# Attention block in fp32: Q and K as two fp32r parts on four 32-row tiles instead of three bf16 parts on two 64-row tiles, with the order of the scores and of the start changed

## The reference, cut to what matters

```python
def tc_rmsnorm(x, t, gw, gb, bw, bb):
    return (t @ gw.T + gb)[:, None] * x * rsqrt(mean(x * x, -1) + 1e-6) + (t @ bw.T + bb)[:, None]

h = tc_rmsnorm(x, cond, g1w, g1b, b1w, b1b)
q, k, v = h @ Wq.T, h @ Wk.T, h @ Wv.T          # 16 heads of 8
p = softmax(q @ k.T / sqrt(8))
x1 = x + (p @ v) @ Wo.T
h2 = tc_rmsnorm(x1, cond, g2w, g2b, b2w, b2b)
out = x + x1 + (silu(h2 @ gate.T) * (h2 @ hid.T)) @ out_w.T
```

## Time and profile before

| | us |
|---|---|
| median of 3 runs | 257.58 (257.5 to 257.66) |
| the profiled execution, its own time | 257.42 |
| its span in the trace | 255.6 |
| PE busy | 221.2 (87%) |
| DVE busy | 202.9 (79%) |
| ACT busy | 163.3 (64%) |
| POOL busy | 111.9 (44%) |

### The profile page before, as it was taken

One profiled execution on the slowest core, in us unless ns is written; L12 is line 12 of the kernel. 1 busy time (PEld: TensorE's weight loads), 2 busy tenths in 40 slices (PEclk: granted clock), 3 DMA queues, 4 the chain that ended last, 5 costly groups with the idle time before them and its releaser, 6 DMA issues.

```text
span 255.6 us, 8235 instructions
## 1 busy us (share of the span) xinstructions
PE 221.2 (87%) x3048; PEld 177.9 (70%) x3048; DVE 202.9 (79%) x490; ACT 163.3 (64%) x352; POOL 111.9 (44%) x183
## 2 busy tenths in 40 slices
PE   2436777879989999899989999999999999899894
PEld 2314545547667868786878877887888778687894
DVE  4646966897899889889988998899888997565673
ACT  5354658676876686669766777567757655666430
POOL 8323852597265254625381516252623232323320
PEclk9995579999999999999999999999999999999998
DMA  5866601530261026100540045004500000000001
GB/s 162 345 169 147 185 4 28 152 85 3 64 166 27 26 64 164 47 23 19 140 124 0 27 112 152 10 27 114 156 6 26 4 26 3 23 3 24 22 21 44
DMA packets 18819, 18.79 MB, mean 74 GB/s; under 512 B 3644, under 2 KB 17980, under 8 KB 18652
## 3 DMA queue, kind: packets, MB, share of 16 engines
q1 hardware_dynamic: 18252, 17.80, 24.7%
q10 hardware_dynamic: 528, 0.46, 0.8%
HBM read 3.22 MB, written 2.10 MB: 21 GB/s over the span
## 4 chain that ended last, share of the span: by engine, by line
PE 45%; issue 24%; POOL 16%; DVE 9%; ACT 4%; ACTq 1%; POOLq 0%; DVEq 0%
PE proj L489 7%; PE pv L427 6%; PE ffn L320 5%; PE ffn L322 3%; PE ffn L321 3%; PE score L410 3%; DVE nmax L756 3%; POOL inv L923 3%; PE raw L383 3%; POOL qp L915 2%; PE tok L442 2%; POOL xn_lo L936 2%; POOL kp L915 2%; POOL xs L929 2%; PE proj L349 2%
## 5 line engine op out<-in xcount | busy, mean ns | idle before, releaser
L756 DVE TENSOR_REDUCE nmax<-raw 128x8 f32<-128x1024 f32 x61 | 74.2, 1216 | 3.0 <-PE raw L383 2.9
L597 ACT ACTIVATE p_s<-score 128x1024 f32<-128x1024 f32 x64 | 65.5, 1023 | 16.1 <-PE score L410 14.9
L427 PE MATMUL pv<-p_s,va 128*32 128x128 f32 x1024 | 41.7, 280 | 1.8 <-ACT xn L615 1.1
L320 PE MATMUL ffn<-xn_hi,ffn_hi 128*128 128x256 f32 x106 | 34.8, 328 | 1.2 <-POOL xn_lo L936 1.2
L626 ACT ACTIVATE th<-ffn 128x256 f32<-128x256 f32 x53 | 20.3, 384 | 19.6 <-PE ffn L322 19.6
L489 PE MATMUL proj<-ffn_out_s,hT 128*128 128x128 f32 x240 | 31.6, 275 | 0.0
L813 DVE SCALAR_TENSOR_TENSOR gated<-th,ffn 128x256 f32<-128x256 f32 x53 | 22.0, 415 | 12.1 <-ACT th L626 11.7
L427 PEld LDWEIGHTS pv<-p_s,va 128*32 128x32 f32 x1024 | 24.7, 109 | 9.2 <-issue 4.0
L936 POOL TENSOR_TENSOR xn_lo<-xn,xn_hi 128x128 fp32r<-128x128 f32 x32 | 14.7, 460 | 34.6 <-DVE xn_hi L804 34.6
L322 PE MATMUL ffn<-xn_hi,ffn_lo 128*128 128x256 f32 x106 | 29.7, 280 | 0.0
L321 PE MATMUL ffn<-xn_lo,ffn_hi 128*128 128x256 f32 x106 | 29.6, 279 | 0.0
(11 more groups left out here) (130 smaller groups left out, 456.0 us busy)
## 6 DMA issues: line engine op xcount, KB each, us to landing
...
qs<-shift SPq DMA_DIRECT2D x64, 4.0 KB
...
```

What stands on the lines that cost most here:

```text
L320: pe.matmul(dst, w_hi, v_hi, start=True, stop=False)
L427: mm = pe.matmul(pv[VW * j:VW * j + VW, (t % 2) * L:(t % 2 + 1) * L], va[vbuf(g)][:, t // 2, at:at + VW], p_s[:, (BEATS * g + t) % PBUF, p ...
L597: act.activation(p_s[:, n % PBUF, :], score[:], ACT.Exp, scale=SCALE).then_inc(s_exp, 1)
L756: dve.tensor_reduce(heads[:, :, t % 2, :], raw_dst(g, t)[:].rearrange("l (e j m) -> l e j m", e=HALVES, j=HQ), AX.X, ALU.max, negate=True) ...
```

## The change

Q and K are split in two fp32r parts, and three products are stacked: 24 of 32 rows, partition stride 4, in tiles of 32 rows. Even steps use tiles 0 and 1, odd steps tiles 2 and 3. The constant `RAW` goes from -7 to -5, so that a raw step has the parity opposite to the score step of its beat, and from beat 3 on their matmuls are issued in turn, one score, one raw, after the waits of both. `a_middle`, `a_lowest` and two buffers go. A group has 6 transfers of 256 KB. The shift is one fp32r row: one copy in `b_shift`, two DMAs for half a group. The transposed maxima go to the `raw` bank, `MAXT` from -3 to -2, and every fourth raw step waits for the shift copy. The first two batches have a maximum transpose, copy and DMA each (`b_first_maxT`, `b_first_shift`, `first_shift_rows`). `tok` and `ffn` become halves of one tensor `aux`, so that raw steps of the first group can use it. The order ahead of the loop changes on all engines; the clearing of `va[0]` moves from DVE to POOL, and the split of the feed-forward weights from beats 4 and 5 to ahead of the loop. The host orders the heads of Wq and Wk to fit. The core of the diff:

```diff
...
-    PARTS = 3
-    Q_PART = [0, 0, 0, 1, 1, 2]
-    K_PART = [0, 1, 2, 0, 1, 0]
+    PARTS = 2
+    TILES = 4
+    TROWS = 32
+    STRIDE = 4
+    Q_PART = [0, 0, 1]
+    K_PART = [0, 1, 0]
...
-    HALF_ROWS = 64
-    RAW_ROWS = 62
+    RAW_ROWS = TROWS - 1
     SHIFT = RAW_ROWS
...
-    RAW, MAXT = -7, -3
+    RAW, MAXT = -5, -2
+    APART = 3
...
-    SPREAD = BEATS * G + RAW + 1 - FFN
+    SPREAD = BEATS * G + MAXT + 1 - FFN
...
-        qp = sb("qp", [D, 2, PARTS, W], BF16)
-        kp = sb("kp", [D, 2, PARTS, W], BF16)
-        q_rest = sb("q_rest", [D, W])
-        k_rest = sb("k_rest", [D, W])
-        qs = [sb(f"qs{u}", [128, HH, W], BF16) for u in range(NBUF)]
-        ks = [sb(f"ks{u}", [128, HH, W], BF16) for u in range(NBUF)]
+        qp = sb("qp", [D, 2, PARTS, W], F32R)
+        kp = sb("kp", [D, 2, PARTS, W], F32R)
+        qs = [sb(f"qs{u}", [128, HQ, W], F32R) for u in range(NBUF)]
+        ks = [sb(f"ks{u}", [128, HQ, W], F32R) for u in range(NBUF)]
         va = [sb(f"va{u}", [L, NB, HALVES * VROW]) for u in range(VBUF)]
...
-        tok = bank("tok")
-        ffn = bank("ffn")
+        aux = bank("aux", 1024)
+        ffn, tok = aux[:, 0:512], aux[:, 512:1024]
...
         def raw_dst(g, t):
-            return score if g == 0 and t % 2 and t < BEATS - 1 else raw
+            return (raw, score, aux, raw, aux, raw, aux, raw)[t] if g == 0 else raw
+        def raw_free(g, t):
+            return BEATS * g + t if g > 0 else (0, 0, 0, 1, 3, 4, 5, 6)[t]
+        def first_maxT(b):
+            return proj[0:H, 0:L] if b == 0 else pv[0:H, 3 * L:4 * L]
...
-                        sp.dma_start(dst[buf(g)][r::DH, :, :].rearrange("p h w -> p (h w)"),
-                                     parts[:, g % 2, part, :]).then_inc(s_stack[buf(g)], 16)
+                        sp.dma_start(dst[buf(g)][r::STRIDE, :, :].rearrange("p j w -> p (j w)").bitcast(F32),
+                                     parts[:, g % 2, part, :].bitcast(F32)).then_inc(s_stack[buf(g)], 16)
             def shift_rows(g, half):
+                sp.wait_ge(s_shift, 2 * g + half if g > 0 else half)
                 for b in range(MB):
-                    for i, ready in enumerate((s_shi, s_slo)):
-                        sp.wait_ge(ready, 2 * g + half + 1)
-                        sp.dma_start(qs[buf(g)][SHIFT + i::HALF_ROWS, :, (MB * half + b) * L:(MB * half + b + 1) * L],
-                                     shift[H * b:H * (b + 1), half, i, :]).then_inc(
-                                         s_shiftrow[buf(g)][MB * half + b], 16)
+                    sp.dma_start(qs[buf(g)][SHIFT::TROWS, :, (MB * half + b) * L:(MB * half + b + 1) * L].bitcast(F32),
+                                 shift[H * b:H * (b + 1), half, :].bitcast(F32)).then_inc(
+                                     s_shiftrow[buf(g)][MB * half + b], 16)
+            def first_shift_rows(b):
+                sp.wait_ge(s_shift0, b + 1)
+                sp.dma_start(qs[0][SHIFT::TROWS, :, b * L:(b + 1) * L].bitcast(F32),
+                             shift_first[:, b, :].bitcast(F32)).then_inc(s_shiftrow[0][b], 16)
...
                 stack_rows(g, ks, kp, K_PART, 0, s_khi)
-                if g == 0:
-                    stack_rows(g, ks, kp, K_PART, 1, s_kmid)
-                    stack_rows(g, ks, kp, K_PART, 2, s_klo)
-                    stack_rows(g, qs, qp, Q_PART, 1, s_qmid)
-                else:
-                    stack_rows(g, qs, qp, Q_PART, 0, s_qhi)
-                    stack_rows(g, ks, kp, K_PART, 1, s_kmid)
-                    stack_rows(g, ks, kp, K_PART, 2, s_klo)
-                    stack_rows(g, qs, qp, Q_PART, 1, s_qmid)
-                stack_rows(g, qs, qp, Q_PART, 2, s_qlo)
+                stack_rows(g, ks, kp, K_PART, 1, s_klo)
+                stack_rows(g, qs, qp, Q_PART, 0, s_qhi)
+                stack_rows(g, qs, qp, Q_PART, 1, s_qlo)
...
-            stack(1)
-            shift_rows(0, 0)
+            one_rows(0)
+            one_rows(1)
+            stack_rows(0, ks, kp, K_PART, 0, s_khi)
+            stack_rows(0, ks, kp, K_PART, 1, s_klo)
+            stack_rows(0, qs, qp, Q_PART, 1, s_qlo)
+            stack_rows(1, ks, kp, K_PART, 0, s_khi)
+            first_shift_rows(0)
+            stack_rows(1, ks, kp, K_PART, 1, s_klo)
+            stack_rows(1, qs, qp, Q_PART, 0, s_qhi)
+            stack_rows(1, qs, qp, Q_PART, 1, s_qlo)
+            first_shift_rows(1)
...
+            def first_key():
+                pe.wait_ge(s_wlo, 1)
+                for n in range(2):
+                    half = slice(2 * n * L, 2 * (n + 1) * L)
+                    pe.wait_ge(s_lo1, n + 1)
+                    mm = split_product(key_dst(0)[:, half], qk_hi[:, 1, :], qk_lo[:, 1, :], xn1_hi[:, half],
+                                       xn1_lo[:, half])
+                mm.then_inc(s_k, 1)
...
+                if raw_free(g, t) > 0:
+                    pe.wait_ge(s_max, raw_free(g, t))
+                if g > 0 and t % HQ == 0:
+                    pe.wait_ge(s_shift, 2 * g - 1 + t // HQ)
...
+            def b_raw_two(g, t):
+                raw_ready(g, t)
+                raw_ready(g, t + 1)
+                for j in range(HQ):
+                    for e in range(HALVES):
+                        first = raw_pair(g, t, e, j)
+                        if j == HQ - 1 and e == HALVES - 1:
+                            first.then_inc(s_raw, 1)
+                        second = raw_pair(g, t + 1, e, j)
+                second.then_inc(s_raw, 1)
...
+            def c_score_and_raw(g, t, f, r):
+                score_ready(g, t)
+                raw_ready(f, r)
+                for j in range(HQ):
+                    for e in range(HALVES):
+                        mm = score_pair(g, t, e, j)
+                        if j == HQ - 1 and e == HALVES - 1:
+                            mm.then_inc(s_score, 1)
+                        nn = raw_pair(f, r, e, j)
+                nn.then_inc(s_raw, 1)
+            def b_maxT(g, half):
+                pe.wait_ge(s_max, BEATS * g + HQ * (half + 1))
+                pe.transpose(raw[:, 0:L], nmax[g % 2][:, half * 128:half * 128 + 128],
+                             ident[:]).then_inc(s_maxT, 1)
+            def b_first_maxT(b):
+                pe.wait_ge(s_max, 2 * (b + 1))
+                if b == 0:
+                    pe.wait_ge(s_va, 1)
+                else:
+                    pe.wait_ge(s_klo, 2)
+                pe.transpose(first_maxT(b), nmax[0][:, H * b:H * (b + 1)], ident[:]).then_inc(s_maxT0, 1)
             def c_pv(g, t, T):
...
-            a_key(0)
+            first_key()
             a_query(0)
             for b in range(NB):
                 a_transpose(1, b)
+            a_values(0)
+            b_raw_two(0, 0)
             a_key(1)
+            b_raw_two(0, 2)
+            b_first_maxT(0)
+            for b in range(NB):
+                a_transpose(2, b)
             a_query(1)
-            b_raw(0, 0)
-            b_raw(0, 1)
-            b_raw(0, 2)
-            b_raw(0, 3)
-            b_raw(0, 4)
-            b_maxT(0, 0)
-            b_raw(0, 5)
-            a_transpose(2, 0)
-            a_transpose(2, 1)
-            a_values(0)
-            a_transpose(2, 2)
-            b_raw(0, 6)
-            a_transpose(2, 3)
             for T in range(LAST + 1):
                 for g, t in due(T, 0, BEATS):
-                    c_score(g, t)
-                for g, t in due(T, RAW, BEATS):
-                    b_raw(g, t)
+                    if T >= APART and due(T, RAW, BEATS):
+                        c_score_and_raw(g, t, *due(T, RAW, BEATS)[0])
+                    else:
+                        c_score(g, t)
+                if T == 0:
+                    b_first_maxT(1)
+                    b_raw_two(0, HQ)
                 for g, t in due(T, PV, BEATS):
                     c_pv(g, t, T)
+                if 0 < T < APART:
+                    for g, t in due(T, RAW, BEATS):
+                        b_raw(g, t)
...
-            a_middle(0, s_krest, k_rest, kp, s_kmid)
             a_high(0, s_q, query_dst(0), qp, s_qhi)
-            a_norm(1, 0)
-            a_norm(1, 1)
-            a_middle(0, s_qrest, q_rest, qp, s_qmid)
             stack_high_queries()
-            a_norm(1, 2)
-            a_norm(1, 3)
+            for b in range(NB):
+                a_norm(1, b)
+            a_values(0)
+            a_mean(2)
+            zero_fill(va[1][:].rearrange("l b v -> l (b v)"), s_va0[1])
             a_high(1, s_k, key_dst(1), kp, s_khi)
+            a_mean(3)
+            for b in range(NB):
+                a_norm(2, b)
             a_high(1, s_q, query_dst(1), qp, s_qhi)
-            a_middle(1, s_krest, k_rest, kp, s_kmid)
-            a_middle(1, s_qrest, q_rest, qp, s_qmid)
-            a_mean(2)
-            a_mean(3)
-            zero_fill(va[1][:].rearrange("l b v -> l (b v)"), s_va0[1])
-            a_norm(2, 0)
-            a_norm(2, 1)
-            a_values(0)
```

(65 more changed lines are left out.)

200 lines of the change are left out of this document (87 added, 113 removed).

## The result

The change makes the kernel slower: median 263.72 us (263.30 to 265.27, four runs) against 257.62 (257.50 to 257.85, four runs), a ratio of 1.0245 [1.0213, 1.0276]. The forecast was 246.0 (238 to 260). (In all ratios an execution over 1.5% above its kernel's fastest is left out; medians and ranges hold all.)

The account below looks back on a forecast made before the run. PE was taken to bound the late beats, with waits between engines early. -9.0 - 2.0 - 2.3 - 0.8 + 2.5 = -11.6 from 257.42 gave 245.8, median 246.0 us; range 238 to 260 with two rivals, own range 238 to 252.

Parts of the forecast that it names:

- The clock: PE's clock could stay low longer, with less PE work before the first scores; taken as within the range, no own term.
- The start: Up to the fifth score: earlier products, transfers and shifts bring it at 36.8 instead of 45.79 us, -9.0 (-5 to -11).
- Beats 4 to 10: Work leaving POOL, ACT and DVE shortens this stretch from 15.4 to about 13.4 us: -2.0 (0 to -3.5).
- Scores and raw scores in one stream: Four rounds at 110 ns make 0.50 instead of 0.55 us a beat, over 46 beats: -2.3 (-0.9 to -3.7).
- Rivals 1: Narrow fp32r matmuls cost what fp32 costs, 0.22 us, so rounds take twice as long: 270 us; chance 0.17.
- rival 2: Weight load not hidden behind its own tile's matmul: 163 ns a round, 257 us, no change; chance 0.10.
- 4 (loads in turn): Weight loads in different tiles go one after another: 1.7 us a beat, over 300 us; chance 0.03.
- Stalls in the late beats: Late groups: shorter POOL and ACT queues gain, the raw, maximum, transpose, copy chain costs; net -0.8 us (-3 to +2).
- The end: Last beats: longer raw scores, slower scores alone, later bank rotation and a late shift add +2.5 us (+1 to +4).
- Rival 3: Early start swallowed: DVE, not PE, binds beats 4 to 16 and half the gain is lost: 252 us; chance 0.10.

Follow-up runs that it names:

- e11: Changed kernel plus 76 filler matmuls (128 rows, results unused) in PE's waits and beats 0 to 9; 253.81 us, ratio 0.9855 to the kernel before.
- e5: Changed kernel with its new order and start, but three bf16 parts on two 64-row tiles and raw scores issued behind the scores; 261.94 us.
- e9: Kernel before with only the new tiles and fp32r parts, keeping the old order and leads; 261.80 us.
- e4: Changed kernel with a beat's eight scores issued first, then its eight raw scores, instead of in turn; 262.92 us.
- e8: Changed kernel plus 78 filler matmuls on 128 rows, in the first stack's wait, behind the first maxima transpose and in beats 0 to 9; 256.21 us.
- e12: As e11 but without any filler matmuls in beats 4 to 9; 258.98 us.

## Why the prediction was wrong

**The clock, the step that failed.** The sum priced the narrow fp32r work at full-clock rows: 110 ns a round in all beats, and beats 4 to 10 by the waits of before, whose clock was 1.00 there. Of the clock it said only that it could stay low longer and that this was "within the range". No term and no rival stood for it. Measured by e11 against the changed kernel: 262.1 - 251.7 = 10.4 us of span, with the cost of e11's fillers still in it. That alone turns -11.6 into -1.2. It is the whole price of the low clock in this kernel, and not only of what the change added to it, since the kernel before was at low clock for some 17 us too. The sign of the evidence was in the earlier trace rows already: 0.71 granted in the start. I took it as a property of the start's idle time, which an earlier start would shorten; the idle time was shortened, and the clock was low for 48 us instead of 17.

**The start.** Up to the first score each step came as worked out: raw scores 18.64, no wait of key(1) for POOL, one transfer's wait of 3.15, first score 25.62. From there the chain was read wrongly, at either clock. I let the fifth score follow from the rows of the second half's shift: last maximum at 33.6, rows at 36.8. In e11, at full clock, that maximum ends at 33.04 + 1.23 = 34.3 and the transpose starts at 34.32, close to it. But behind it PE's queue holds the key product, beat 3 and the query product:

```profile
34.32 0.33 PE L469 MATMUL raw<-ident,nmax 128*128 128x128 f32 x1 [0.42 <-DVE nmax L817]
...
36.67 1.22 PE L563 MATMUL aux<-qk_hi 128*128 128x256 f32 x8
...
39.15 0.40 PE L336 MATMUL proj<-xn_hi,qk_lo 128*128 128x512 f32 x1
39.48 0.32 PE L425 MATMUL score<-qs,ks 32*128 32x128 f32 x1
```

The fifth score starts at 39.48, set by PE's own order and not by the shift, without an idle gap in front of it; 0.9 of that are the eight fillers of beat 3. I had named what is queued behind the stalled transpose and then not added it: 2.7 us. At half clock the same chain reaches 44.6. There the eighth raw product comes late as well; DVE's timeline of the changed kernel:

```profile
31.07 1.22 DVE L801 TENSOR_REDUCE nmax<-aux 128x8 f32<-128x1024 f32 x1 [0.58 <-PE aux L405]
36.28 1.23 DVE L801 TENSOR_REDUCE nmax<-raw 128x8 f32<-128x1024 f32 x1 [3.98 <-PE raw L405]
```

**Beats 4 to 10.** Forecast -2.0, measured +7.0. The larger part is the clock: e11 takes 17.1, of which twelve fillers are at most 1.3. That leaves 15.8 or more, so with the clock full nothing is gained either. The forecast took work off POOL, ACT and DVE (POOL did fall from 10.99 us to 6.75 in e11) and let the stretch shrink with it; it is a chain of waits between engines in which none of them was the bound, and e5, with bf16, shows 15.5. Work removed from engines that waited most of the time was worth nothing in this stretch.

**Scores and raw scores in one stream.** The round was right, about 110 ns, set by the load, and so was the reading that loads in four tiles run beside each other. Rivals 1 (over 200 ns), 2 (163) and 4 (loads in turn) are refuted by the same rows: in one tile the loads start 0.10 to 0.11 us apart (106.49, 106.60, 106.70), so the matmul between two of them adds nothing to the load's 107 ns. A load half as long, with its matmul not hidden, would give 110 as well; against it, a load in a 32-row tile is recorded with 0.18 to 0.19 us, like one on 128 rows (0.19). The rule that I had cited beside rival 2 from the Trainium skill, "TensorE: Matmul & The Clock Gate", section "Part 3: Packing small matmuls" (a load overlaps only where the row groups differ), does not hold here: it would give 163 ns, and the trace has 110. The ends were mis-sized. The first round is 0.17 from the second instead of 0.11 and the last 0.21 from PV instead of 0.15 to 0.20: 0.60 instead of 0.50, so +0.05 a beat against before instead of -0.05. Over the 40 beats from 16 to 56 this is +2.0; PE's busy time rose by 128.41 - 127.01 = 1.4. Sixteen fp32r matmuls on four tiles cost a little more than sixteen in bf16 on two.

**Stalls in the late beats.** Forecast -0.8. Time in which PE isn't busy fell from 131.3 - 127.0 = 4.3 to 131.6 - 128.4 = 3.2, so -1.1, right, and in both of its parts: e9, without the new chain, has 130.4 - 128.9 = 1.5, so the work that POOL and ACT lost is worth -2.8 and the new order +1.7. With bf16 parts (e5) the new order costs 2.5 in such time, above the bound of +2 for the whole.

**The end.** Forecast +2.5, measured +1.1: eight scores alone last 0.66 instead of 0.40, as worked out. PE's busy time from beat 56 to the end rose by 1.9 (37.4 to 39.3), and 0.8 less of waiting took it up. With the tiles alone (e9) the stretch is 43.5, with the new order alone (e5) 44.2, against 43.2 before: the narrow tiles cost little here and the order most.

**Rival 3** (DVE binds beats 4 to 16) would have given 252. DVE is busy for 12.21 of 21.8 us after: it waits, for PE at half clock.

Put together: of the 18.1 us between forecast and measured span, 10.4 are the clock. The other 7.7 stand even in e11, its fillers in these beats included: 2.7 to the fifth score, 3.7 in beats 4 to 10 (17.1 instead of 13.4), 2.6 in beats 10 to 56 (150.7 instead of 148.1), less 1.3 at the end.

**What stays open.** The best mix was not tried: new tiles with the old leads have the shortest late beats of all (130.4), the new start with fillers the shortest start. Why bf16 parts lose 3.8 us with the new leads and fp32r parts 1.2 was not isolated. The kernel before was given fillers only in beats 3 to 9, not from 18.4 to 38.9, where its own clock is low for 17 us, so what e11 gains over it may be open to it as well. Traces were read of one execution each, and e4, e8 and e12 show that the clock differs between executions. Nor was the change's start tried with real work in place of the fillers, for example the weight split or the third group's products moved into the wait.
